# Six gather tiles of a pass fetched row by row from two DMA queues, instead of three tiles of one group

## What is computed

```python
x = layernorm(x + L0(x))                 # weighted messages, two small linear maps
# L1: ten steps; L2: sixteen steps of the same kind
def spmm(feat):
    msg = feat[col] * w[:, None]         # 25000 gathered rows of 96 numbers
    return segment_sum(msg, row, n)      # summed by target node
for _ in range(10):                      # L1
    out = spmm(out) * 0.9 + h * 0.1
for _ in range(16):                      # L2, with degree norms and self loops
    h = 0.9 * segment_sum(norm * h[row], col, n) + 0.1 * x
x = layernorm(x + L3(x))                 # two convolutions with a PReLU
```

## Time and profile before

| | us |
|---|---|
| median of 3 runs | 8946.5 |
| the three runs | 8943.17, 8946.5, 8952.78 |
| span of the profiled execution | 8950.4 |

### The profile page before, as it was taken

The page is one execution under the profiler, slowest core; times in us unless marked ns, Lnnn a source line. Parts: engine busy times, 40 slices in busy tenths (PEclk is TensorE's granted clock), DMA queues, the critical chain, the costliest instruction groups (busy, mean ns, idle before and its releaser), DMA issues. The chain is left out here.

```text
span 8950.4 us, 111450 instructions
## 1 busy us (share of the span) xinstructions
PE 5474.2 (61%) x23642; PEld 4375.0 (49%) x23642; DVE 4879.1 (55%) x12173; ACT 1977.2 (22%) x5359; POOL 6658.3 (74%) x7008
## 2 busy tenths in 40 slices
PE   7566644444454443346777777877666667766643
PEld 6465533333333332225666666655555556555543
DVE  7687555555555556755555555544444444465444
ACT  2355631111111110633111111100000000056433
POOL 6677677777777777677777777777777777777777
PEclk9777755555555555557777777776777767665555
DMA  7664544444444443434444444443333334333311
GB/s 145 133 178 124 95 108 106 107 105 106 110 113 108 106 102 97 138 72 103 112 112 113 114 115 114 119 104 98 99 98 97 99 97 103 94 98 88 83 45 37
DMA packets 905581, 939.53 MB, mean 105 GB/s; under 512 B 380578, under 2 KB 796456, under 8 KB 904806
## 3 DMA queue, kind: packets, MB, share of 16 engines
q1 hardware_dynamic: 652430, 588.73, 22.0%
q0 software_dynamic: 223680, 320.10, 18.9%
q10 hardware_dynamic: 28794, 23.58, 0.9%
HBM read 560.22 MB, written 399.35 MB: 107 GB/s over the span
## 5 line engine op out<-in xcount | busy, mean ns | idle before, releaser
L1924 POOL DMA_INDIRECT l_g<-tab,l x2898 | 2737.2, 945 | 895.3 <-issue 830.4
L2129 DVE TENSOR_TENSOR_SCAN l_w<-l_m,l_w,bank 96x512 f32<-96x512 bf16 x1248 | 1591.9, 1276 | 2707.3 <-PE bank L1956 2690.3
L1956 PE MATMUL bank<-ident,l_g 128*96 128x128 f32 x5030 | 1171.1, 377 | 1887.8 <-DMA l_g<-tab,l 919.3
L1924 POOL DMA_INDIRECT l_g<-tab,XM x1740 | 1651.0, 949 | 530.7 <-issue 481.4
L1956 PEld LDWEIGHTS bank<-ident,l_g 128*96 128x96 f32 x5030 | 756.2, 172 | 2339.4 <-DMA l_g<-tab,l 1035.7
L1976 PEld LDWEIGHTS bank<-ident,l_w 96*128 96x128 f32 x6272 | 1602.7, 328 | 324.8 <-issue 252.4
L1976 PE MATMUL bank<-ident,l_w 96*128 96x96 f32 x6272 | 1507.1, 401 | 6.8 <-DVE l_w L2129 6.4
L1967 PE MATMUL bank<-XM,ident 128*128 128x384 f32 x1568 | 921.1, 681 | 0.0
L2046 ACT ACTIVATE T<-T,dinv_e 128x96 f32<-128x96 f32 x196 | 57.0, 361 | 1968.2 <-DVE T L2154 1966.2
L419 ACT ACTIVATE tail_y<-bank,tail_of,tail_sc 125x96 f32<-125x96 f32 (+1 forms) x596 | 208.7, 431 | 1236.1 <-DVE tail_of L410 1229.5
L308 PE MATMUL bank<-tail_xt,v 96*96 96x500 f32 (+1 forms) x298 | 275.3, 1025 | 316.0 <-ACT tail_xt L303 316.0
(11 more groups left out here) (330 smaller groups left out, 9739.4 us busy)
## 6 DMA issues: line engine op xcount, KB each, us to landing
tab<-T SPq DMA_DIRECT2D x784, 192.0 KB
row_buffer<-tab ACTq DMA_DIRECT2D x5808, 0.4 KB
tab<-l_o SPq DMA_DIRECT2D x441, 192.0 KB
l_m<-mask_d SPq DMA_DIRECT2D x784, 96.0 KB
l_m<-mask_s SPq DMA_DIRECT2D x490, 96.0 KB
l_g<-tab,l POOLq DMA_INDIRECT x2898
row_buffer<-tab SPq DMA_DIRECT2D x2640, 0.4 KB
l_g<-tab,XM POOLq DMA_INDIRECT x1740
```

The costliest lines, as they stand in the source:

```text
L1924: nc.gpsimd.indirect_dma_start(out=tile(G[q % RG], t), out_offset=None, in_=tables[0:table_at + (2 - p % 2) * TR, :] if p else first, in_o ...
L1956: last = nc.tensor.transpose(a_bank(q)[0:D, u:GE:U], rows[:, u * D:(u + 1) * D], self.ident[:, :])
L2129: v.tensor_tensor_scan(out=W[q % RW][:, :], data0=masks[q % RM][:, :], data1=a_bank(q)[0:D, :], initial=W[(q - 1) % RW][:, GE - 1:GE] if q ...
```

## The change

The row-wise share is laid out anew. In the same 22 passes the last tile (`ROW_U` = 3) of each of the six groups 11, 18, 25, 32, 39 and 46 comes row by row: 768 transfers in a pass. Each tile's 128 rows are shared, 56 on SP and 72 on ACT; SP issues eight in a group and ACT eleven, from group 2 on, so SP has a tile's rows out after every seven groups and the last in group 43, and ACT has its last in group 41. POOL leaves out one gather in each of the six groups, and group 45 has its four again. The extra step of `AHEAD_GROUPS` behind group 45 is gone.

The index is multiplied by 384 once for each layer (by VectorE, `row_bytes`), so registers hold byte addresses and line 1817 with its register arithmetic is gone; the transfer is written as 384 elements of one byte. A register load brings 16 (for the last of a tile 8). Each tile has its own semaphore `rows_in`, so a turn waits only for its own 128 rows.

```diff
-ROW_GROUP, ROW_TILES, ROW_FROM, ROW_LOAD = NGP - 4, 3, 2, 8
-ROWS = P * ROW_TILES
-ROW_SHARES = {"sp": (0, 120, 3), "act": (120, ROWS, 7)}
+ROW_GROUPS = {"power": tuple(range(11, 47, 7)), "smooth": tuple(range(11, 47, 7))}
+ROW_U, ROW_FROM, ROW_LOAD, ROW_BYTES = U - 1, 2, 16, 4 * D
+ROW_SHARES = {"sp": (0, 56, 8), "act": (56, P, 11)}
...
-        return 16 * (U * (at // RG + 1) - ROW_TILES * fetched)
+        return 16 * (U * (at // RG + 1) - fetched)
...
             def keep_index(sp):
-                tiles = slice(ROW_GROUP * U, ROW_GROUP * U + ROW_TILES)
-                with nc.allow_non_contiguous_dma(reason="three numbers of each partition"):
+                sp.wait_ge(self.index_scaled, self.index_loads)
+                with nc.allow_non_contiguous_dma(reason="some numbers of each partition"):
                     for k in range(2):
-                        sp.dma_start(index_row(k).rearrange("a (p u) -> (a p) u", u=ROW_TILES), later[k][:, tiles]
+                        sp.dma_start(index_row(k).rearrange("a (u p) -> (a p) u", p=P), row_bytes(k)
                                      ).then_inc(self.index_out, 16)
...
-                for k in range(n, min(n + each, end)):
-                    if k % ROW_LOAD == 0:
-                        eng.load(self.row_at[kind], self.row_index[index:index + 1, k:k + ROW_LOAD])
-                    row = eng.snap(self.row_at[kind][k % ROW_LOAD])
-                    u = k % ROW_TILES
-                    eng.dma_start(self.row_buffer[k // ROW_TILES:k // ROW_TILES + 1, u * D:(u + 1) * D],
-                                  table[bass.ds(row, 1), :]).then_inc(self.rows_in[kind], 16)
+                for k in range(n, min(n + each, some * len(row_groups))):
+                    j, at = k // some, k % some
+                    if at % ROW_LOAD == 0:
+                        count, col = min(ROW_LOAD, some - at), j * P + begin + at
+                        part = 2 * index + col // GE
+                        eng.load(self.row_at[kind][0:count],
+                                 self.row_index[part:part + 1, col % GE:col % GE + count])
+                    first_byte = bass.RuntimeValue.of_register_unchecked(
+                        self.row_at[kind][at % ROW_LOAD], min_val=0, max_val=(rows - 1) * ROW_BYTES)
+                    eng.dma_start(into[begin + at:begin + at + 1, j * ROW_BYTES:(j + 1) * ROW_BYTES],
+                                  flat[bass.ds(first_byte, ROW_BYTES)].rearrange("(a d) -> a d", a=1)
+                                  ).then_inc(self.rows_in[j], 16)
...
-                        back = 1 if out_rows and g > LAG else AHEAD_GROUPS + by_rows(q - 1)
+                        back = 1 if out_rows and g > LAG else AHEAD_GROUPS
...
-                        for t in range(g * U + ROW_TILES * by_rows(q), (g + 1) * U):
+                        for t in range(g * U, (g + 1) * U - by_rows(q)):
...
                     if by_rows(q):
-                        for n, (begin, end, _) in ROW_SHARES.items():
-                            pe.wait_ge(self.rows_in[n], 16 * (end - begin))
-                            pe.sem_clear(self.rows_in[n])
+                        j = row_groups.index(q % NGP)
+                        pe.wait_ge(self.rows_in[j], 16 * P)
+                        pe.sem_clear(self.rows_in[j])
...
+                if looped:
+                    apart = U * (row_groups[1] - row_groups[0])
+                    columns = slice(row_groups[0] * U + ROW_U, row_groups[-1] * U + ROW_U + 1, apart)
+                    for k in range(2):
+                        v.tensor_single_scalar(row_bytes(k), later[k][:, columns], ROW_BYTES, op=ALU.mult
+                                               ).then_inc(self.index_scaled, 1)
```

More of the change, by code:

```diff
@@ L1718, in passes @@
         if looped:
[L1719 removed]
+            row_groups = ROW_GROUPS[mode]
+            self.by_row |= {self.groups + own + p * NGP + g for p in range(1, final) for g in row_groups}
             self.index_loads += 2
```

42 lines of the change are left out of this document (27 added, 15 removed).

## The result

| | before | changed | difference |
|---|---|---|---|
| median, us | 8949.64 | 8882.85 | -66.8 |
| lowest and highest, us | 8943.17, 8955.06 | 8876.75, 8909.66 | |
| ratio, 95% interval | | 0.9933 | 0.9921 to 0.9945 |
| predicted, us | | 8866 (8856 to 8902) | -80 |

There are four runs of each kernel. The profiled execution of the changed kernel is the slowest of its four, 8909.66 us with a span of 8907.8. So the time is in the range and on the side that was forecast, and the gain is 16 us short of the 82 that the sum had for the gathers.

A forecast was written before the change was run, and what follows sets the result against it. POOL's gathers were taken as the bound: the median before, 8946.5 us, less 82.4 for gathers left out, plus 2 for preparation, gave 8866 us. Range 8856 to 8880, with two slower rivals up to 8902.

The forecast's parts named there:

- A gather less is worth 1.248 us: POOL's queue: three gathers fewer in each of 22 passes, 66 x 1.248 = 82.4 us saved.
- rivals 2 and 3: Two slower cases, queues saturating a little and PE as bound; they raised the range's top to 8902 us.
- Preparation: VectorE multiplies and index copies in 768 pieces at each layer's start: 2 us for both layers, bounds 0 and 10.
- Rows at no cost: Row transfers on SP and ACT, and POOL's wait for landings behind short groups, priced at nothing if the queues keep up.
- gaps over 0.4 us behind short groups: Sign of a wrong forecast on POOL: such gaps, where 0.30 was expected.
- Loads and pitches: Load of sixteen about 1.2 us; rows 0.316 us apart on ACT, 0.347 on SP; ACT 170 to 190 us a pass.
- When rows are due: SP's last rows, three groups before their turn: 9.3 us needed against 14.5, a margin of 5.2 us.
- one of the prediction's signs of being wrong: Sign on PE: its turn waiting for `row_buffer`, the rows fetched by SP and ACT.
- The first: SP becomes the bound because a load of sixteen costs more than in proportion: 8986 us, chance 7%.
- The second: Queues saturate a little, a few late tiles in seven smoothing passes with tails: 20 to 40 us lost, chance 14%.
- The third: PE bounds the smoothing passes with tails, whose saving of 26 us is lost: 8892 us, chance 5%.
- The fourth: Gathers landing 0.6 us later than a short group lasts hold POOL, the gain gone: 8947 us, chance 5%.

The follow-up runs named there:

- before_prep: Kernel before the change plus only its preparation: four multiplies and two index copies in 768 four-byte pieces a layer; 8961.86 us, ratio 1.0015.
- read_back: Changed kernel with row numbers written out in 128 pieces of 24 bytes and put in tile order when read back; 8876.6 us, ratio 0.9916.
- again: The changed kernel unaltered, measured a second time beside the kernel before; 8883.62 us, ratio 0.9932.
- strided: Changed kernel with index copies in 24-byte pieces and register loads picking every sixth number; 9729.94 us, ratio 1.088.
- word_addr: Changed kernel with row numbers instead of byte addresses in registers, so register arithmetic precedes each row again; 9115.15 us, ratio 1.0181.
- load8: Changed kernel with eight numbers a register load instead of sixteen on both SP and ACT; 8945.89 us, ratio 0.9995.
- load8_act: Changed kernel with eight numbers a register load on ACT alone, sixteen on SP; 8940.8 us, ratio 0.9985.
- sp48: Changed kernel with eight rows of each tile moved from SP to ACT (48 on SP, 80 on ACT); 8914.31 us, ratio 0.9956.

## Why the prediction was right, and where its steps were off

**A gather less is worth 1.248 us: right.** 3.7 and 3.8 us a pass without the rows, for three gathers, in both layers. The ends of the passes are as before, so the shorter pass moves all that follows.

**Where the number lies.** The forecast without rivals went from 8856 to 8880, and 8882.85 is just outside; it is in the full range only by the part that was added for rivals 2 and 3, and neither happened. What used that room up are the next two terms.

**Preparation: mis-sized.** The step put 2 us with an upper bound of 10; `before_prep` has 10.4 us in two stretches, and `read_back` takes 8.1 of them away again. The step scaled the landing of a copy by its pieces, 6 x 2.8 = 17 us, and saw correctly that nobody waits for the numbers. The landing is 9.7 us, and it wasn't the numbers but the gathers in flight beside it that were late: the 11 GB/s stretch. The step asked who waits for the transfer and not what the transfer does to POOL's.

**Rows at no cost: mis-sized.** They were priced at nothing as long as the queues keep up. They cost about 13 us, 1.2 in a power pass and 0.25 in a smoothing pass. About half of that is the wait that the prediction weighed and priced at nothing: a landing of 2 us behind the end of a gather, against a short group of 3.74. With rows the landing takes 2.9 us behind the end in the power layer (3.8 from the start), and POOL goes on 0.76 us after it, at group 29 2.97. Its own sign of being wrong, gaps over 0.4 us behind short groups, is there in a few passes.

**The sum with measured terms:** -82.4 + 10 + 13 = -59, beside -62.8 for `again` and -66.8 for the first set; the terms come from single profiles. Together they are more than what the gain lacks of the forecast of 80, by 4 us for `again` and 8 for the first set.

**Loads and pitches: right within the bounds.** 1.3 to 1.4 us for sixteen (1.2 taken, 0.83 to 1.65 given). ACT's 432 rows span 183.0 us in a pass without tails of `again`, in the bounds of 170 to 190:

```profile
L1837 ACTq DMA_DIRECT2D row_buffer<-tab x432: 219/220/526, 6291.8 to 6474.8; - x144
```

The Trainium skill's page "Runtime: NRT & Kernel Launch", section "Instruction fetch mechanics", with about 200 ns a register, is not borne out by these loads: sixteen in a row take 1.3 us and not 3.2. The 3.7 us of `strided` are near its figure, but for numbers that lie apart.

**When rows are due: the margin was smaller.** 5.2 us were worked out for tile 46, with 2 for the landing already taken off; the last eight rows of SP in `again` end at 4529.95 and the turn is at 4532.1, so 2.2 us remain, and the landing has to fit in. The step took the turn, the scan and SP's own work for all that stands ahead of the last rows. What it left out is that PE, and with it the scan that SP's mask load waits for, can itself be held by ACT. In the power layer the margin was used up: PE waits 3.3 to 7.6 us for the rows of tile 46 in each of the eight passes, and twice more in the last of them. This is one of the prediction's signs of being wrong. From the table of waits of `again` over that layer (total, times, longest), where the kernel before has 0.4 us:

```profile
PE bank L1977 <- DMA row_buffer<-tab: 42.5, 10, 7.6
```

It cost nothing at the ends of these passes: 29.0 us stand between two of them with the 23 own gathers, and 15.3 behind the last, as before.

**The rivals.** The first (slower, loads too dear) didn't happen in the change, but `strided` and `word_addr` show PE waiting for `row_buffer`. In `word_addr` it is as described: a smoothing pass with tails and its end take some 20 us more than before, a power pass 2.8, the rest being covered by the own gathers. In `strided` the power passes pay 35 us each too. The second (the queues saturate a little, tiles late in passes with tails) didn't happen either, since the ends of the smoothing passes with tails are 11.6 us as before, but `load8`, `load8_act` and `sp48` show that 16 to 18 us a pass more on ACT's queue bring it about. The prediction had SP as the tighter queue and called ACT safe because 190 + 44 = 234 us fit in a pass. The sum was right, and the conclusion was not: ACT's tail steps have to be in time one by one, and PE waits for each. The third (PE) shows in part: its reserve fell from 260 to 159 us, but it isn't the bound. The fourth (gathers land late) came about in small: in the power layer they land 0.7 us later than before, and the waits for them come to some 7 us more than without rows, not to the whole gain.

## What to carry to other kernels

Ask of a side transfer not only who waits for it but what it does to the transfers beside it: here one copy in pieces of four bytes held the bottleneck engine up for 4 to 6 us, and cutting it into twelve made it worse, while writing the same bytes in pieces of 24 and reordering on the way back removed 8 of the 10 us. When work is moved to a queue that seems to have room, add up not only its time but the latest moment of every short step that now stands behind it, and look at the reserve of the engine that waits for those steps; loads of eight instead of sixteen registers cost nearly all that the change had gained.

## What the runs showed of the chip that was not expected

- Copies from the chip to HBM in pieces of four bytes land after 8.0 to 11.0 us (medians of the kernels), be they 128, 384 or 768 pieces, and in `again` the traffic was down to 11 GB/s for 8 us beside them; in pieces of 12 or 24 bytes they land after 2.5 to 3.3. Reading in pieces of four bytes cost 1 us at most.
- On ACT a register load of sixteen neighbouring numbers takes 1.3 us, of eight 0.83, so 0.36 us plus 0.06 a register; with numbers six apart it is 3.7 us.
- Single-row transfers from SP and ACT beside POOL's gathers made the gathers of the power layer land later: the last of a group 3.8 us after its start, against 2.9 without the rows.
- Two executions of the same kernel differ in the pace of a gather on POOL, 944 or 947 ns in the median over the whole span, which makes 14 of the 21 us between their spans. A profile that is slower by some tenths of a per cent can owe most of it to no single place.
- Open: why POOL goes on 2.97 us after the landing that it waits for ahead of group 29, and 0.76 us elsewhere.
